# Attention core on one Trainium2 core: maxima and scores issued two by two in every second block, read together by VectorE, with the halves of the array alternating

## The reference

```python
def _L0_attn_ref(x, w_q, s_q, b_q, w_k, s_k, b_k, w_v, s_v, b_v, w_o, s_o, b_o):
    ...
    q = split_heads(_tlin(x, w_q, s_q, b_q))
    k = split_heads(_tlin(x, w_k, s_k, b_k))
    v = split_heads(_tlin(x, w_v, s_v, b_v))
    scores = jnp.einsum('bhqd,bhkd->bhqk', q, k) / jnp.sqrt(jnp.float32(HEAD))
    attn = jax.nn.softmax(scores, axis=-1)
    ctx = jnp.einsum('bhqk,bhkd->bhqd', attn, v)
    ctx = ctx.transpose(0, 2, 1, 3).reshape(B, S, H)
    return _tlin(ctx, w_o, s_o, b_o)
...
x = _layernorm(x + _L0_attn_ref(x, ...), axis=-1)
x = _layernorm(x + _L0_ffn_ref(x, L0_ffn_w_gate, L0_ffn_w_up, L0_ffn_w_down), axis=-1)
```

## Time and profile before

| | |
|---|---|
| median of 3 runs | 1981.41 us (1981.15 to 1986.02) |
| profiled execution | 1983.3 us, span 1981.5 us |
| TensorE, busy | 1931.0 us, 97% |
| VectorE, busy | 1845.4 us, 93% |
| ScalarE, busy | 1652.1 us, 83% |
| granted TensorE clock, mean | 0.997 |

### The profile page before, as it was taken

How to read it: one execution, slowest core, us unless ns; L and a number is a source line. 1 busy time by engine, 2 the same in 40 slices (tenths; PEclk the granted TensorE clock), 3 DMA queues, 4 the chain that set the end, 5 groups by cost and what they waited for, 6 DMA issues and landing times.

```text
span 1981.5 us, 43034 instructions
## 1 busy us (share of the span) xinstructions
PE 1931.0 (97%) x15806; PEld 1131.4 (57%) x15806; DVE 1845.4 (93%) x3236; ACT 1652.1 (83%) x3241; POOL 750.0 (38%) x747
## 2 busy tenths in 40 slices
PE   8999999999999999999999999999999999999998
PEld 7766444444444444444444444444478888888876
DVE  4788999999999999999999999999289999999997
ACT  6655889899898989989898988988967777777776
POOL 3000364666575353010001001000046666666785
PEclk9999999999999999999999999999999999999999
DMA  7985553355435435433543544353011111111210
GB/s 224 284 236 209 120 76 52 62 95 96 94 81 102 95 80 99 93 94 82 101 96 78 97 94 94 82 100 98 28 49 49 49 49 49 49 49 56 63 33 27
DMA packets 127199, 181.46 MB, mean 92 GB/s; under 512 B 37836, under 2 KB 82636, under 8 KB 126988
## 3 DMA queue, kind: packets, MB, share of 16 engines
q1 hardware_dynamic: 119308, 171.10, 37.6%
q10 hardware_dynamic: 7392, 7.34, 1.1%
q0 software_dynamic: 288, 0.27, 0.1%
HBM read 103.68 MB, written 73.40 MB: 89 GB/s over the span
## 4 chain that ended last, share of the span: by engine, by line
DVE 63%; PE 32%; issue 3%; DMA 1%; ACT 1%; SPq 0%; DVEq 0%; POOLq 0%; POOL 0%; ACTq 0%
DVE halfmax L1135 50%; PE ps L1401 10%; DVE halfmax L1130 7%; PE ps L1440 6%; PE ps L494 4%; PE ps L504 3%; PE ps L1389 2%; PE ps L1412 2%; PE ps L1045 1%; PE ps L1011 1%; PE ps L481 1%; PE ps L1448 1%; DVE room L1591 1%; PE ps L1457 1%; DVE room L1678 1%
## 5 line engine op out<-in xcount | busy, mean ns | idle before, releaser
L1096 ACT ACTIVATE room<-ps 128x512 f32<-128x512 f32 x2048 | 1084.4, 600 | 125.0 <-PE ps L1011 103.0
L1135 DVE TENSOR_REDUCE halfmax<-ps 128x1 f32<-128x512 f32 x1714 | 1039.5, 676 | 1.3 <-PE ps L986 1.3
L1011 PE MATMUL ps<-qs,ks 50*128 50x512 f32 x2048 | 716.4, 448 | 2.4 <-DVE halfmax L1135 1.3
L986 PE MATMUL ps<-ks,qs 48*128 48x512 f32 x1960 | 667.6, 437 | 23.8 <-DVE halfmax L1130 22.3
L1045 PE MATMUL ps<-room,vals 128*17 128x256 f32 (+2 forms) x8192 | 578.9, 384 | 0.3 <-ACT craw L1104 0.3
L986 PEld LDWEIGHTS ps<-ks,qs 48*128 48x128 f32 x1960 | 314.5, 185 | 423.6 <-DVE halfmax L1135 309.2
L164 POOL CAST mrow<-turned_rows 128x32 fp32r<-128x32 f32 x32 | 6.7, 210 | 904.2 <-DVE turned_rows L159 695.4
L1011 PEld LDWEIGHTS ps<-qs,ks 50*128 50x128 f32 x2048 | 327.2, 184 | 22.9 <-ACT room L1096 14.5
L1045 PEld LDWEIGHTS ps<-room,vals 128*17 128x17 f32 x8192 | 167.4, 96 | 232.9 <-issue 168.1
L1401 PE MATMUL ps<-wguT,xqT 128*128 128x512 f32 (+1 forms) x1152 | 268.4, 386 | 3.9 <-DVE xqT L1631 3.9
L1401 PEld LDWEIGHTS ps<-wguT,xqT 128*128 128x128 f32 x1152 | 212.0, 189 | 51.8 <-issue 9.9
(11 more groups left out here) (116 smaller groups left out, 2212.1 us busy)
## 6 DMA issues: line engine op xcount, KB each, us to landing
qk_parts<-parts SPq DMA_DIRECT2D x64, 512.0 KB, 3.9
qs<-qk_parts SPq DMA_DIRECT2D x192, 128.0 KB, 4.4
ks<-qk_parts SPq DMA_DIRECT2D x192, 128.0 KB, 7.1
ctx_raw<-craw SPq DMA_DIRECT2D x64, 256.0 KB
ready<-passing SPq DMA_DIRECT2D x27, 512.0 KB, 6.5
pairs<-ready SPq DMA_DIRECT2D x27, 512.0 KB
out_dram<-fin SPq DMA_DIRECT2D x64, 128.0 KB, 1.7
xin<-in_L_attn_x_dram ACTq DMA_DIRECT2D x14, 512.0 KB, 5.4
```

Source lines behind the costliest of these rows:

```text
L986: nc.tensor.matmul(ps[:, MX + max_number(i, u, bank) % 4, :], qs[rows, i.slot(RING), pair, t * P:(t + 1) * P], ks[rows, i.slot(RING), pair ...
L1011: nc.tensor.matmul(ps[:, score_bank(i, s, n), :], ks[rows, slot, pair, kt * P:(kt + 1) * P], qs[rows, slot, pair, qh * BANK:(qh + 1) * BAN ...
L1096: nc.scalar.activation(prob[:, prob_slot(i, s), score_order(i, s)[n], :], ps[:, score_bank(i, s, n), :], ACT.Exp, scale=float(D) ** -0.5). ...
L1135: nc.vector.tensor_reduce(halfmax[:, i.slot(2), bank, column:column + 1], ps[:, at + bank, :], AX.X, ALU.max, negate=True).then_inc(max_re ...
```

## The change

In every block of three that starts at an odd tile (`side_by_side`), TensorE first issues a maxima tile and a score tile, as before, then two maxima tiles, then two score tiles. VectorE reads those two maxima tiles with one instruction (`TOGETHER`); no others are read so. That makes five double reads in 32 tiles, in place of two: maxima tiles 0/1, 8/9, 14/15, 20/21 and 26/27. For the two to lie in opposite halves, the order of the maxima tiles is changed (`max_tile_at`: the half alternates from tile to tile, and the two halves of the keys come two tiles apart), and so is the order of the score tiles (`SCORE_ORDER` 1, 0, 3, 2: their half alternates too). A double read now yields the maxima of two heads for one half of the keys. `whole_max` comes behind the first maxima read of its step, the transpose behind the third tile.

```diff
-SCORE_ORDER = (1, 3, 0, 2)
-ALONE_ORDER = (1, 0, 3, 2)
+SCORE_ORDER = (1, 0, 3, 2)
...
-def max_tile_at(u):
-
-    return u % 2, (u // 2) % GP, u // GH
-
-
-def max_column(u):
-    half, pair, t = max_tile_at(u)
-    return (half * GP + pair) * (S // P) + t
+def max_tile_at(v):
+
+
+    return v % 2, (v // 2) % QH, (v // GH) % GP, v // (2 * GH)
...
-    WHOLE = (0, 7)
-
-    def whole(i, u):
-
-        return item[i.k, u] % (2 * KT) in WHOLE
-
-    def max_number(i, u, bank):
-
-
-        return QH * item[i.k, u] + bank
+    def max_number(i, v):
+
+
+        return QH * (MU * (i.k - 1) - LEAD) + v
+
+    def side_by_side(tiles):
+
+
+
+        return len(tiles) == 3 and tiles[1] % 2 == 0 and tiles[0] >= GH
+
+    TOGETHER = {tiles[1] - GH for tiles, quarters in blocks() if side_by_side(tiles)}
...
+        def max_tile(tile):
+
+
+            step, n = divmod(tile, GH)
+            if step == 0:
+                return
+            i, first = maxima(*step_at(step - 1))
+            v = first + n
+            if v == 0:
                 pe.wait_ge(stack_in[i.slot(RING)], i.turn(RING, LOADS, LOADS))
-            if max_number(i, u, bank) >= 4:
-
-                pe.wait_ge(max_read, reads_done[max_number(i, u, bank) - 4])
-            half, pair, t = max_tile_at(u)
+            if max_number(i, v) >= 4:
+
+                pe.wait_ge(max_read, reads_done[max_number(i, v) - 4])
+            half, bank, pair, t = max_tile_at(v)
...
         for tiles, quarters in blocks():
-            for tile in tiles:
-                max_and_score(tile)
+            if side_by_side(tiles):
+                max_tile(tiles[0])
+                score_tile(*score_at(tiles[0]))
+                for tile in tiles[1:]:
+                    max_tile(tile)
+                for tile in tiles[1:]:
+                    score_tile(*score_at(tile))
+            else:
+                for tile in tiles:
+                    max_tile(tile)
+                    score_tile(*score_at(tile))
...
+        def take_max(i, v):
+            number = max_number(i, v)
+            half, bank, pair, t = max_tile_at(v)
+            column, at = pair * (S // P) + t, MX + number % 4
+            maxima_of = halfmax[:, i.slot(2), bank].rearrange("p (a n) -> p a n", a=2)
+            if number in TOGETHER:
+                dve.wait_ge(max_psum, number + 2)
+                nc.vector.tensor_reduce(maxima_of[:, :, column:column + 1], ps[:, at:at + 2, :], AX.X, ALU.max,
+                                        negate=True).then_inc(max_read, 1)
+            else:
+                dve.wait_ge(max_psum, number + 1)
+                nc.vector.tensor_reduce(maxima_of[:, half, column:column + 1], ps[:, at, :], AX.X, ALU.max,
+                                        negate=True).then_inc(max_read, 1)
```

More of the change, by code:

```diff
@@ L840, in blocks, with score_at @@
             quarter = end
+    def score_at(tile):
+        return *step_at(tile // GH), tile % GH
     def step_at(step):
@@ L853, in paired @@
         return number(i, s) > BARE
-    def score_order(i, s):
-        return ALONE_ORDER if paired(i, s) else SCORE_ORDER
     def score_bank(i, s, n):
@@ L872, in scores_due @@
         return s * GH + n - (len(BARE_BANKS) if paired(i, s) else SRING) + 1
[L874 to L880, removed]
-    WHOLE = (0, 7)
-    def whole(i, u):
-        return item[i.k, u] % (2 * KT) in WHOLE
-    def max_number(i, u, bank):
-        return QH * item[i.k, u] + bank
-    def read_table():
[L897 to L903, removed]
+    def max_number(i, v):
[3 more added lines that the diff above has]
+    TOGETHER = {tiles[1] - GH for tiles, quarters in blocks() if side_by_side(tiles)}
+    def read_table():
+        table, last = [], max_number(At(None, NGR - 1, RING), QH * MU)
+        while len(table) < last:
+            reads = table[-1] if table else 0
+            table += [reads + 1] * (2 if len(table) in TOGETHER else 1)
         return table
@@ L914, in maxima @@
         if s < ST - AHEAD:
-            return i.plus(1), 2 * (s + AHEAD)
-        return i.plus(2), 2 * (s - (ST - AHEAD))
+            return i.plus(1), GH * (s + AHEAD)
+        return i.plus(2), GH * (s - (ST - AHEAD))
     def sync(sp):
@@ L975, in tensor @@
     def tensor(pe):
-        def max_bank(i, u, bank):
-            if u == 0 and bank == 0:
+        def max_tile(tile):
[5 more added lines that the diff above has]
+            if v == 0:
                 pe.wait_ge(stack_in[i.slot(RING)], i.turn(RING, LOADS, LOADS))
-            if max_number(i, u, bank) >= 4:
-                pe.wait_ge(max_read, reads_done[max_number(i, u, bank) - 4])
-            half, pair, t = max_tile_at(u)
+            if max_number(i, v) >= 4:
+                pe.wait_ge(max_read, reads_done[max_number(i, v) - 4])
+            half, bank, pair, t = max_tile_at(v)
             rows = slice(half * HALF, half * HALF + KR)
-            nc.tensor.matmul(ps[:, MX + max_number(i, u, bank) % 4, :],
+            nc.tensor.matmul(ps[:, MX + max_number(i, v) % 4, :],
                              qs[rows, i.slot(RING), pair, t * P:(t + 1) * P],
@@ L1008, in score_tile @@
             qh, kt = divmod(s, KT)
-            pair, half = divmod(score_order(i, s)[n], 2)
+            pair, half = divmod(SCORE_ORDER[n], 2)
             rows = slice(half * HALF, half * HALF + KM)
@@ L1014, in score_tile @@
                              start=True, stop=True).then_inc(score_psum, 1)
[L1016 to L1024, removed]
         def values(step, quarters):
@@ L1095, in exps @@
                 act.wait_ge(score_psum, i.lin(ST * GH, s * GH + n + 1))
-                nc.scalar.activation(prob[:, prob_slot(i, s), score_order(i, s)[n], :],
+                nc.scalar.activation(prob[:, prob_slot(i, s), SCORE_ORDER[n], :],
                                      ps[:, score_bank(i, s, n), :],
@@ L1144, in whole_max @@
                                     for a in (negmax[:, i.slot(RING)], halfmax[:, i.slot(2), 0], halfmax[:, i.slot(2), 1]))
-            dve.wait_ge(max_read, reads_done[max_number(i, MU - 1, QH - 1)])
+            dve.wait_ge(max_read, reads_done[max_number(i, QH * MU - 1)])
             nc.vector.tensor_tensor(whole, first, second, ALU.min).then_inc(max_whole, 1)
@@ L1168, in vector @@
                 j, first = maxima(i, s)
[L1169 to L1181, removed]
+                for v in range(first, first + GH):
+                    if j.ok(NGR) and max_number(j, v) - 1 not in TOGETHER:
+                        take_max(j, v)
+                    if s == ST - AHEAD and i.ok(NGR - 1):
+                        if v == 0:
+                            whole_max(i.plus(1))
+                        if v == 2:
+                            dve.wait_ge(max_whole, i.lin(1, 1))
+                            maxima_out.turn(nc, dve, negmax, i.plus(1))
         fill.vector(dve, range(FILL))
```

## The result

| | before | changed |
|---|---|---|
| median of 5 runs | 1981.41 us (1979.92 to 1986.02) | 1992.11 us (1990.89 to 1995.61) |
| profiled execution, span | 1981.5 us | 1989.4 us |
| single reads | 1714 | 1350 |
| double reads | 123 | 305 |

The changed kernel is slower by 0.53% (ratio 1.0053, interval 1.0037 to 1.0069). The forecast was 1992. The interval stands for 7.3 to 13.7 us more, the forecast for 10.7.

The account below looks back on a forecast made before the run. VectorE was taken to set the pace, TensorE up to four banks ahead. Per 64 maxima tiles 0.48 + 0.34 - 0.08 - 0.39 = +0.35 us, times 30.6 is 10.7, on 1981.4: 1992 us, range 1976 to 2002.

Parts of the forecast that it names:

- The gain of 0.065 us for a merge: VectorE: a double read replaces two singles, 1.13 for 2 x 0.598 us; 0.39 us saved per 64 maxima tiles.
- the one late read of before: Kernel before, tile 19 after double read 14/15: VectorE reads it 0.08 us late, once in 64 maxima tiles.
- The loop of 3.60: Double read to double read, four singles on: TensorE's path makes it 3.60 us, 0.08 over VectorE's own 3.52.
- The rival in which VectorE stays fed: Path through the value matmuls 0.08 shorter, loop 3.52 us: 1967 us, or 1973 for half; chance 0.14.
- The two loops that pay nothing: Two of eight loops per 64 tiles: VectorE's other work fills the 0.08 us, so six pay, 0.48.
- The copy: ScalarE's copy between exponentials 5 and 6 makes tile 7 late by 0.17 us, twice in 64 tiles: 0.34.
- the rival in which the copy is absorbed: Loops as computed, ScalarE's copy costs nothing: 0.40 loss against 0.39 gain, 1981 to 1984 us; chance 0.23.
- The long sum: Path from tile 3's matmuls to tile 7: readable at 5.44 us, wanted at 5.25, late by 0.19.
- T: Start of tile 3's matmuls on TensorE, from which the prediction counted times up to tile 7.
- like pairs: Two maxima or two score matmuls in opposite halves start together like unlike pairs: no cost, at most 0.24 us per pair.
- late scores: Rival: side-by-side block's second score comes 0.24 us later, ScalarE falls behind: 25 us, 2017 us; chance 0.06.
- The rival of the same-half boundary: TensorE pairs beginning in the half where the last ended show a 0.18 us weight load: 64 us more, 2056; chance 0.04.

Follow-up runs that it names:

- e6: Changed kernel with interleaved order (maxima, score, maxima, score) in every block, new halves kept, and no double reads: 1988.62 us, ratio 1.0034 to the kernel before.
- e1: Changed kernel with only its alternating halves kept: interleaved order in every block, double reads at 0 and 14 of 32 as before: 1981.78 us, ratio 0.9999.
- e4: Changed kernel with interleaved order in every block and double reads moved to maxima tiles 4, 10, 16, 22, 28 of 32: 1966.99 us, ratio 0.9913.
- e2: Changed kernel with TensorE's order put back to maxima, score, maxima, score in every block, its five double reads kept: 1992.46 us, ratio 1.0046.
- e3: Changed kernel with its side-by-side order kept, but double reads only at maxima tiles 0 and 14 of 32, as before: 1982.59 us, ratio 1.0000.
- e5: Changed kernel with ScalarE copying only 32 of 512 columns, except in the first two copies (results wrong): 1983.7 us, ratio 1.0002 to the kernel before.

## Why the prediction was right

- **The gain of 0.065 us for a merge.** Right. It is in the start-to-start distances of the changed kernel (706.29 - 705.16 = 1.13), and e6 against e1 has it at the scale of the whole run. Had nothing else moved, 11.8 us would have come; e4, with one more double read, gained 15.3 against the kernel before beside it (1982.3). The merges and the one late read of before make 11.9 + 2.4 = 14.3, which lies inside the interval (13.9 to 20.6 us).
- **The loop of 3.60.** Right in mechanism and size: 3.61 to 3.62 in the trace. The rival in which VectorE stays fed asked for 3.52 and is out. e2 and e3 show that the double reads cause the loss and not the order of issue, e4 that it is their place and not their number. That the path runs from the double read's end over the third tile of the next block and the value matmuls is read from the timeline, and e4 moved exactly this; no run shortened the value matmuls or the block themselves.
- **The two loops that pay nothing.** By the mean over the groups, the single read at the end of the loop was late by 0.04 us (maxima tiles 13 and 19, the ones with other work every second time) and by 0.08 us (25 and 31): 0.48 for 64 tiles, as the sum had it.
- **The copy.** The mechanism was right, and the rival in which the copy is absorbed is out by e5. The size was too large: 0.34 for 64 tiles was taken, tile 7 was late by 0.143 twice, 0.29. As an experiment, e5 gives 8.4 us for 30.6 groups, 0.27 each. The long sum came to 0.19 each time, of which the prediction took 0.17; it was off by small pieces on both sides. In the rows above, with T at 707.63, tile 10's score starts at T + 3.69 and tile 7 is read at T + 5.42, where the prediction had 3.7 and 5.44; and the double read 0/1 starts at T + 1.15 and not 1.13, so that tile 7 is wanted at 5.27 and not 5.25.
- **What was left out.** The read behind a late one starts 0.61 and not 0.598 behind it (708.78 - 708.17). That is 0.01, eight times a group, 0.08 us, once of which the kernel before had too.
- **The sum, and luck.** With the terms as measured it is 0.48 + 0.29 + 0.08 - 0.09 - 0.39 = 0.37 us a group, 11.3 us in all; the copy term was 0.05 too large and the 0.01s, which the prediction put at nothing, more than make up for it. The stretch of the single reads grew by 12.0 us, where 10.7 were forecast. What lies outside that stretch, which the change doesn't touch, took 799.1 us in this trace and 803.2 before; over the traces of all runs it moves between 797.9 and 805.6. Terms of the right kind put the forecast within 1 or 2 us; that 1992.11 meets 1992 to a tenth is luck, and beside the later median of 1982.3 the same kernel is 9.8 us slower.
- **Halves, like pairs, late scores.** The rival of the same-half boundary is out by e1 (its price was 64 us). In the Trainium skill ("TensorE: Matmul & The Clock Gate", "Part 3: Packing small matmuls") a weight load overlaps matmuls in flight only in another row group; here the trace does not agree. The loads of 0.19 us for the next pair start at 707.74, while the matmuls of 0.50 us that started at 707.63 and 707.64, one in each half, are in flight, and the pair's matmuls follow at 707.98. For this kernel the measurement decides against a price. Late scores are out too: e2, which has none of them, took 1992.46 against 1992.11, less apart than the 0.15% to which either ratio is known.
- **What would have shown it.** The prediction asked for 5 to 10 us of idle ahead of single reads, released by the maxima matmuls. There were 5.7, but only 1.6 of them are put down to these matmuls, and 1.3 were before: the reading by releaser is weaker than the reading by distances. The other signs came as asked: 305 double and 1350 single reads, 3.62 us from double to double, and a stretch that is longer by 12.0 us, where 10 were named.

## What to carry to other kernels

When an engine that looks busy without a hole is sped up by larger instructions, ask where each of its buffers comes free and follow that release through the other engine's program back to the next instruction: a larger read holds its banks longer, and its place among the other engine's blocks decides whether that closes a loop. Measure such a loop from start to start, since lateness shorter than the overlap of one instruction with the next (0.08 us here) appears nowhere as idle time. Here five double reads in 32 tiles lost 0.5% at maxima tiles 0, 8, 14, 20 and 26, and gained 0.9% at 4, 10, 16, 22 and 28.

## What the runs showed of the hardware

A read that had to wait for its tile (duration 0.69 in the rows of 704.55 and 708.17) is followed 0.61 us later, 0.01 more than the 0.598 of an unbroken stream. I had not expected it. The single reads in e4's stream last 0.68 and start 0.598 apart all the same.
